# Attention heads taken in pairs: weight transposes, value products and their copies for two heads at once, query products two steps ahead

## The chip, the cores and the metric

The kernel runs on one core of a Trainium2 chip. The metric is the device time of one execution in microseconds (us), lower is better. Five engines with queues of their own work side by side and meet only at semaphores: TensorE (PE; its weight loads are shown apart as PEld), VectorE (DVE), ScalarE (ACT), GpSimd (POOL) and SyncE (SP, which issues most DMAs). Each engine takes its instructions strictly in the order in which they were written.

## The reference

Input x is 16 batches of 256 rows of 512 numbers. Four layers are added to it one after the other: a long convolution with gating, a mixture of experts, cross attention, and a dense feed-forward layer. Only the attention is touched here:

```python
kv_c = kv @ W_kvc                     # 256 x 128 per batch
q_c = q @ W_dq                        # 256 x 192
q_nope = (q_c @ W_uq)                 # 16 heads x 128
q_rope = rope(q_c @ W_qr)             # 16 heads x 64
scores = (q_nope . (kv_c @ W_uk) + q_rope . rope(kv_c @ W_kr)) * scale
scores = where(good, scores, -1e30)   # 8 keys back from the segment id
attn = softmax(scores)
out = (attn . (kv_c @ W_uv)) @ W_o    # summed over the 16 heads
```

## The kernel before, in words

The attention phase folds weights, so that a head needs four steps on TensorE. `scores` multiplies the absorbed query (`qah`, `qal`, 128 rows) and the rotated query (`qr`, a high and a low half) with the keys: ten products into bank `S` for both query tiles. `pturn` transposes the softmax weights `pr` (four transposes into bank `T`). `av` multiplies them with the compressed values (six products into bank `PO`). `vo` multiplies the result with the folded output weight (six products, 512 wide, into the two banks `U`). Every operand is kept as a rounded high part and a low part: ScalarE copies the bank into the high part, VectorE subtracts it from the bank to get the low part (`pth`/`ptl`, `oth`/`otl`, `qah`/`qal`). So each step on TensorE is followed by a copy on ScalarE and, behind it, one subtraction on VectorE.

The queries are prepared beside this. `qabs(P)` makes the absorbed queries of two heads (ten products). `qrot(Q, t)` makes the rotated queries of four heads for one query tile: five products, three multiplications on VectorE and an addition on GpSimd. `qrot2` splits the sum into `rr` (a copy on ScalarE, then a subtraction on VectorE), and `qturn` transposes `rr` (four transposes) and ScalarE copies the result to `qr`.

The order is written out by hand in one loop over N = 16 b + h (b the batch, h the head, 256 steps and four to drain). Each step issues, in this order: `qrot2` where it is due, `scores(N)` (with VectorE's masked minimum `L1224` and ScalarE's exponent `L1228` for two tiles), `qrot` where it is due, `vo(N-4)`, the preparation of the next batch (lists `Bq`), `normalise(N)` (`L1234`, `L1235`), `pturn(N-1)`, `av(N-2)`, `wprep` (only in the first eight steps), and the list `C` with `qturn` and `qabs`. The preparation of batch b+1 in step h: statistics at 0 and 1, normalising at 1 and 2, transposes at 2 and 3, the mask at 4 (eight VectorE instructions), `keys` at 5, `values` at 6, `krope` at 7, `qcomp` at 9; GpSimd mixes the input of batch b+2 (`mix`, four long instructions) after steps 12 and 14. The output of a batch is added on VectorE (`L1275`) at step 3 of the next.

Three PSUM banks (`M0` to `M2`) are handed out in turn by `take()`; whoever takes one waits for the release by the taker three before. The last steps also start the dense layer (`next(dense)`). The conversion of the weights to head factors (`wprep`) fills the start of the attention, where GpSimd mixes batch 1, SyncE stores it, and VectorE's `norm(1, 0)` waits for that store.

Of the kernel before, what the change touches and what calls it, by code (L numbers as in the profile page):

```python
# [926 lines left out]
def attention_phase(nc, ctx, mem, d, front, idx, gat, ident, mhalf, small, batches=B):  # L927
# [282 lines left out]
    def scores(N):  # L1210
# [10 lines left out]
        for t in range(2):  # L1221
# [6 lines left out]
            T["ex", x] = p.do("scalar", lambda e, t=t, k4=k4: e.activation(pr[:, N % 2, t, :], sm[:, k4, :], ACT.Exp, bias=nb[:, k4, 0:1], scale=-1.0,  # L1228
                                                                           accum_out=rw[:, k4, 0:1]), am, g("pt", N - 2), g("rc", x - 4))

    def normalise(N):
# [4 lines left out]

    def pturn(N):
        for kb in range(2):
            for t in range(2):
# [4 lines left out]
        T["pth", N] = p.do("scalar", lambda e: e.activation(pth[:, N % 2, :, :], v, ACT.Copy), a, g("av", N - 2))  # L1244
        T["ptl", N] = p.do("vector", lambda e: e.tensor_tensor(ptl[:, N % 2, :, :], v, f32(pth[:, N % 2, :, :]), ALU.subtract), T["pth", N], g("av", N - 2))  # L1245

    def av(N):
        b, h = divmod(N, NH)
        s = b % 2
        i = 0  # L1250
        for kb in range(2):
# [4 lines left out]
        T["av", N] = a
        v = PO[:, 256 * (N % 2):256 * (N % 2) + 256]
        T["oth", N] = p.do("scalar", lambda e: e.activation(oth[:, N % 3, :], v, ACT.Copy), a, g("vo", N - 3))
        T["otl", N] = p.do("vector", lambda e: e.tensor_tensor(otl[:, N % 3, :], v, f32(oth[:, N % 3, :]), ALU.subtract), T["oth", N], g("vo", N - 3))
# [20 lines left out]
    prf = pr[:, :, :, :].rearrange("p a b c -> p (a b c)")  # L1280
# [104 lines left out]
    T["pt", -1] = T["pt", -2] = T["f", 7]  # L1385
    total = batches * NH
    for N in range(total + 4):
        b, h = divmod(N, NH)
        A, Bq, C = [], [], []
# [19 lines left out]
        for f in A:  # L1409
            f()  # L1410
# [315 lines left out]
```

How the kernel before makes its waits and increments, by code:

```python
    def emit(self, e, eng):  # L72
        seen = {}
        def wait(sem, v):
            if seen.get(id(sem), 0) < v:
                eng.wait_ge(sem, v)
                seen[id(sem)] = v
        for sem, v in self.before:
            wait(sem, v)
        for fn, waits, inc in self.q[e]:
            for w in waits:
                if w is not None:
                    wait(*w)
            ins = fn(eng) if fn else None
            if inc:
                ins.then_inc(*inc)
# [1616 lines left out]
                def run(eng, e=e):  # L1705
                    for p in phases:
                        p.emit(e, eng)
                    if e == "sync":
                        for sem, v in before:
                            eng.wait_ge(sem, v)
```

## Time and profile before

| | us |
|---|---|
| median of 3 runs | 3246.66 (3245.66 to 3248.66) |
| the profiled execution | 3243.99 |
| its span | 3242.2 |
| TensorE busy over the span | 3145.1 (97%) |
| VectorE busy | 2159.4 (67%) |
| ScalarE busy | 1258.5 (39%) |
| GpSimd busy | 1124.4 (35%) |

The attention runs from 1156.75 (first `scores` product) to 2517.71 (first product of the dense layer). A product on TensorE is pipelined: what one costs is the distance from start to start, not its own duration, which overlaps the next. The same holds in part for VectorE and ScalarE. Waits of an engine that is not the bottleneck cost nothing.

### The profile page before, as it was taken

What the parts mean: (1) busy time and instruction counts of PE and PEld (TensorE: products, weight loads), DVE (VectorE), ACT (ScalarE), POOL (GpSimd) and SP (SyncE); (2) the same over time, 40 slices, a digit from 0 to 9 for tenths busy, and PEclk for the clock granted to TensorE, in tenths of its full rate; (3) what the DMA queues carried; (4) which work ended last, traced back from release to release, by engine and by line L of the source; (5) the groups of instructions that cost most, each with busy time, mean ns of one, the idle gap of its engine ahead of it and who ended that gap; (6) DMA issues with size and microseconds to landing.
All of it is one profiled execution on the core that took longest, in us unless ns stands there. A gap on an engine that the chain in (4) does not pass through costs nothing.

```text
span 3242.2 us, 51534 instructions
## 1 busy us (share of the span) xinstructions
PE 3145.1 (97%) x18517; PEld 2686.6 (83%) x18517; DVE 2159.4 (67%) x5741; ACT 1258.5 (39%) x3041; POOL 1124.4 (35%) x1176
## 2 busy tenths in 40 slices
PE   7999999999999789999999999999999999999999
PEld 4666666688899669999999999999999788888887
DVE  6888888755555568888877787777788533333332
ACT  2333333333344345555555555555555311111111
POOL 6877777625344322222222222222211111001110
PEclk9999999999999899999999999999999999999999
DMA  4445443259777731111111111111110300000000
GB/s 128 147 140 149 130 130 102 78 177 335 224 228 230 240 103 53 47 40 40 47 47 36 44 47 47 47 46 47 40 34 21 114 33 26 27 27 26 26 14 14
DMA packets 129418, 285.92 MB, mean 88 GB/s; under 512 B 18840, under 2 KB 19488, under 8 KB 129168
## 3 DMA queue, kind: packets, MB, share of 16 engines
q1 hardware_dynamic: 100080, 186.49, 18.3%
q0 software_dynamic: 29088, 96.13, 9.0%
q8 instruction: 153, 2.51, 0.3%
q14 instruction: 97, 0.79, 0.1%
HBM read 177.98 MB, written 104.58 MB: 87 GB/s over the span
## 4 chain that ended last, share of the span: by engine, by line
PE 78%; DVE 10%; POOL 7%; DMA 2%; ACT 1%; issue 1%; SPq 0%; POOLq 0%; DVEq 0%
PE g_O L1533 11%; PE g_PH L1514 11%; PE t_U L1266 10%; PE t_S L1218 9%; PE t_PO L1253 5%; PE t_M L1202 5%; POOL c_kf L355 3%; PE t_T L1240 3%; PE f_Y L893 3%; PE f_Y L664 2%; PE t_M L1157 2%; PE f_Y L387 2%; PE f_Y L382 2%; DVE c_R L400 2%; DVE c_z L394 2%; PE t_M L1139 2%
## 5 line engine op out<-in xcount | busy, mean ns | idle before, releaser
L1228 ACT ACTIVATE t_pr<-t_sm,t_nb 128x256 f32<-128x256 f32 x512 | 256.5, 502 | 375.0 <-DVE t_nb L1224 375.0
L1172 POOL TENSOR_TENSOR t_r<-t_r 128x256 f32<-128x256 f32 x128 | 96.0, 750 | 779.9 <-DVE t_rw L1234 452.0
L1523 DVE CAST g_hh<-g_hf 128x512 fp32r<-128x512 f32 x128 | 62.2, 486 | 414.5 <-PE g_O L1533 413.0
L1533 PE MATMUL g_O<-g_w,g_hh 128*128 128x512 f32 x1024 | 335.9, 389 | 0.0
L1514 PE MATMUL g_PH<-g_xh,g_w 128*128 128x512 f32 x1024 | 319.8, 394 | 7.0 <-DVE g_w L109 7.0
L355 POOL TENSOR_TENSOR c_kf<-c_vt,c_ct 128x512 f32<-128x512 f32 x256 | 296.4, 1178 | 0.0
L1522 ACT ACTIVATE g_hf<-g_PH,b1g 128x512 f32<-128x512 f32 x128 | 88.3, 690 | 501.7 <-PE g_PH L1514 501.7
L1235 DVE TENSOR_SCALAR t_pr<-t_pr,t_rw 128x256 f32<-128x256 f32 x512 | 222.9, 435 | 18.1
L1514 PEld LDWEIGHTS g_PH<-g_xh,g_w 128*128 128x128 f32 x1024 | 191.0, 189 | 45.8 <-DVE g_w L109 7.4
L1533 PEld LDWEIGHTS g_O<-g_w,g_hh 128*128 128x128 f32 x1024 | 192.2, 188 | 39.9
L387 PE MATMUL f_Y<-c_kh,c_th 128*128 128x512 f32 x448 | 200.1, 447 | 10.4 <-ACT c_kh L362 10.4
L1266 PE MATMUL t_U<-t_voh,t_oth 128*128 128x512 f32 x512 | 202.0, 395 | 0.0
L1266 PE MATMUL t_U<-t_voh,t_otl 128*128 128x512 f32 x512 | 201.9, 394 | 0.0
L1224 DVE CUSTOM_DVE_ANT_0 t_sm<-t_S,t_mk 128x256 f32<-128x256 f32 x512 | 194.8, 417 | 9.2 <-PE t_S L1218 9.2
L1266 PE MATMUL t_U<-t_vol,t_oth 128*128 128x512 f32 x512 | 200.7, 392 | 0.0
L1514 PE MATMUL g_PH<-g_xl,g_w 128*128 128x512 f32 x512 | 200.3, 391 | 0.0
L1533 PE MATMUL g_O<-g_w,g_hl 128*128 128x512 f32 x512 | 199.2, 389 | 0.0
L394 DVE TENSOR_TENSOR c_z<-f_Y,c_ct 128x512 f32<-128x512 f32 x256 | 174.0, 680 | 34.7 <-PE f_Y L382 34.5
L382 PE MATMUL f_Y<-c_kf,c_t 128*128 128x512 f32 x384 | 185.4, 591 | 0.0
L1245 DVE TENSOR_TENSOR t_ptl<-t_T,t_pth 128x512 fp32r<-128x512 f32 x256 | 175.5, 685 | 11.7 <-ACT t_pth L1244 11.6
L400 DVE TENSOR_REDUCE c_R<-c_z 128x64 f32<-128x512 f32 x256 | 174.9, 683 | 6.7
L387 PE MATMUL f_Y<-c_kl,c_th 128*128 128x512 f32 x448 | 178.1, 397 | 0.0
(335 smaller groups left out, 9319.1 us busy)
## 6 DMA issues: line engine op xcount, KB each, us to landing
xs<-c_zero SPq DMA_DIRECT2D x71, 256.0 KB, 5.3
f_xg<-xs SPq DMA_DIRECT2D x71, 256.0 KB, 3.2
ys<-f_yt POOLq DMA_DIRECT2D x71, 256.0 KB, 3.3
c_tr<-kpad SPq DMA_DIRECT2D x60, 256.0 KB, 4.7
f_xg<-xn SPq DMA_DIRECT2D x40, 256.0 KB
c_xt<-x SPq DMA_DIRECT2D x32, 256.0 KB, 3.5
c_cr<-ctx SPq DMA_DIRECT2D x32, 256.0 KB, 3.9
c_ct<-ctxh SPq DMA_DIRECT2D x32, 256.0 KB, 4.4
```

The source lines that it names most:

```text
L355: T["kv", h] = T["kv1", n] = p.do("gpsimd", lambda e: e.tensor_tensor(o, iv, ic, ALU.mult), g("vt", h), g("ct", h), g("kl", n - 8), g("kh" ...
L382: last = p.do("tensor", lambda e, c=c, mb=mb: e.matmul(Y[y % 4][:, :], t0[:, s, c], kf[:, v, mb, :], start=False, stop=mb == lb), g("t0", ...
L387: last = p.do("tensor", lambda e, a=a, b_=b_, c=c, mb=mb, i=i: e.matmul(Y[y % 4][:, :], a[:, s, c], b_[:, v, mb, :], start=(mb == 0 and i ...
L394: T["z", h] = T["z1", y] = p.do("vector", lambda e: e.tensor_tensor(zz.rearrange("p (b j i) -> p b j i", i=8, j=8), iv, ic, ALU.mult), las ...
L400: T["red", y] = T["R", h] = p.do("vector", lambda e: e.tensor_reduce(rr, zr, AXX, ALU.add), g("z1", y), g("pr", h - 2))
L1218: a = p.do("tensor", lambda e, t=t, j=j, q=q, k=k: e.matmul(PS1[:, 256 * t:256 * t + 256], q, k[:, s, :], start=j == 0, stop=j == 4), g("q ...
L1224: T["am", N] = am = p.do("vector", lambda e, t=t, k4=k4: e.tensor_tensor_reduce(out=sm[:, k4, :], in0=PS1[:, 256 * t:256 * t + 256], in1=m ...
L1228: T["ex", x] = p.do("scalar", lambda e, t=t, k4=k4: e.activation(pr[:, N % 2, t, :], sm[:, k4, :], ACT.Exp, bias=nb[:, k4, 0:1], scale=-1. ...
L1235: T["nm", x] = p.do("vector", lambda e, t=t, k4=k4: e.tensor_scalar(pr[:, N % 2, t, :], pr[:, N % 2, t, :], rw[:, k4, 1:2], None, ALU.mult ...
L1266: a = p.do("tensor", lambda e, t=t, tt=tt, j=j, o=o, w=w: e.matmul(PU[t][:, :], o[:, N % 3, tt], w[:, h, :], start=h == 0 and j == 0, stop ...
L1514: T["ph", n] = p.do("tensor", lambda e, kk=kk, a=a, b_=b_, i=i: e.matmul(ph[:, :], a[k][:, kk, :], b_[:, s, kk, :], start=i == 0, stop=i = ...
L1533: tk = p.do("tensor", lambda e, a=a, b_=b_, t=t, fin=fin, c=c, beg=beg: e.matmul(O[t][:, :], a[:, n % 2, c], b_[k], start=beg, stop=fin), ...
```

## The change

The softmax weights get three buffers instead of two. At every even step N the weight transposes of heads N-2 and N-1 are issued together (the second head's into one of the three shared banks), directly behind the rotated queries' four transposes. `av` runs at every odd step for two heads at once, six products 512 wide in place of twelve 256 wide, with one copy and one subtraction 512 wide in place of two each. `qrot`, `qrot2`, `qturn` and `qabs` move ahead by one or two steps, `qcomp` goes to step 7 and `krope` to step 8; before the loop `qrot(1, 0)`, `qrot(1, 1)` and `qabs(1)` are added, which the loop then lacks. The steps of the dense layer come one step later.

```diff
-    oth = m.sb("oth", [128, 3, 256], F32R)
-    otl = m.sb("otl", [128, 3, 256], F32R)
+    oth = m.sb("oth", [128, 2, 256], F32R)
+    otl = m.sb("otl", [128, 2, 256], F32R)
+    pr = m.sb("pr", [128, 3, 2, 256])
...
     def pturn(N):
+        i = N % 2
+        bank, pi, pf = take() if i else (PT1, None, g("ptl", N - 2))
         for kb in range(2):
             for t in range(2):
-                a = p.do("tensor", ... e.transpose(PT1[...], pr[:, N % 2, t, ...], ident),
-                         g("nm", 2 * N + 1), g("nm", 2 * N), g("ptl", N - 1), c_id, ...)
+                a = p.do("tensor", ... e.transpose(bank[...], pr[:, N % 3, t, ...], ident),
+                         g("nm", 2 * N + 1), g("nm", 2 * N), pf, c_id, ...)
...
+        if i:
+            free_m(pi, T["ptl", N])
     def av(N):
...
-                a = p.do("tensor", ... e.matmul(PO[:, 256 * (N % 2):256 * (N % 2) + 256], k[:, s, kb, :], q[:, N % 2, kb, :], ...
+                a = p.do("tensor", ... e.matmul(PO[:, :], k[:, s, kb, :], q[:, kb, :, :].rearrange("p h c -> p (h c)"), ...
...
-        T["oth", N] = p.do("scalar", ... oth[:, N % 3, :], v ... g("vo", N - 3))
-        T["otl", N] = p.do("vector", ... otl[:, N % 3, :], v ... g("vo", N - 3))
+        T["oth", N] = T["oth", N + 1] = p.do("scalar", ... oth[:, :, :], v ... g("vo", N - 1))
+        T["otl", N] = T["otl", N + 1] = p.do("vector", ... otl[:, :, :], v ... g("vo", N - 1))
...
     qturn(0, 1)
+    qrot(1, 0)
+    qrot2(1, 0)
     qabs(0)
+    qrot(1, 1)
+    qabs(1)
...
+            if 4 * (Q + 2) < total:
+                A += {1: [lambda: qrot(Q + 2, 0)], 2: [lambda: qrot2(Q + 2, 0)], 3: [lambda: qrot(Q + 2, 1)]}.get(r, [])
             if 4 * (Q + 1) < total:
-                A += {0: [lambda: qrot(Q + 1, 0)], 1: [lambda: qrot(Q + 1, 1)]}.get(r, [])
-                if r in (1, 2):
-                    qrot2(Q + 1, r - 1)
-                C += {1: [lambda: qturn(Q + 1, 0)], 2: [lambda: qturn(Q + 1, 1)]}.get(r, [])
-            if N % 2 == 0 and N // 2 + 1 < total // 2:
-                C += [lambda: qabs(N // 2 + 1)]
+                A += {0: [lambda: qrot2(Q + 1, 1)]}.get(r, [])
+                D += {0: [lambda: qturn(Q + 1, 0)], 2: [lambda: qturn(Q + 1, 1)]}.get(r, [])
+            if N % 2 and N + 3 < total:
+                C += [lambda: qabs((N + 3) // 2)]
...
-  ... 7: [lambda: krope(b + 1)], 9: [lambda: qcomp(b + 1)],
+  ... 7: [lambda: qcomp(b + 1)], 8: [lambda: krope(b + 1)],
...
+        if N % 2 == 0:
+            for f in D:
+                f()
+            if 0 <= N - 2 < total:
+                pturn(N - 2)
+                pturn(N - 1)
         if 0 <= N - 4 < total:
             vo(N - 4)
         for f in Bq:
             f()
         if N < total:
             normalise(N)
-        if 0 <= N - 1 < total:
-            pturn(N - 1)
-        if 0 <= N - 2 < total:
-            av(N - 2)
+        if N % 2 and 0 <= N - 3 < total:
+            av(N - 3)
```

Three places where this moves instructions. TensorE, step h = 10 of a batch, from the end of its scores on. Before, the transposes stand behind `vo` and the value products (L1253) directly behind them:

```order
L1218 MATMUL t_S<-t_krl,t_qr 128x256
L1266 MATMUL t_U<-t_voh,t_oth 128x512
L1266 MATMUL t_U<-t_voh,t_otl 128x512
L1266 MATMUL t_U<-t_vol,t_oth 128x512
L1266 MATMUL t_U<-t_voh,t_oth 128x512
L1266 MATMUL t_U<-t_voh,t_otl 128x512
L1266 MATMUL t_U<-t_vol,t_oth 128x512
L1240 MATMUL t_T<-ident,t_pr 128x128 [waits t_vector]
L1240 MATMUL t_T<-ident,t_pr 128x128 x3
L1253 MATMUL t_PO<-t_pth,t_kvh 128x256 [waits t_scalar,t_vector]
```

Now twelve transposes stand in a row ahead of `vo` (L1272), four of rotated queries, eight of weights:

```order
L1218 MATMUL t_S<-t_krl,t_qr 128x256
L1187 MATMUL t_M<-t_identr,t_rr 128x128 x4
L1243 MATMUL t_T<-ident,t_pr 128x128 x4
L1243 MATMUL t_M<-ident,t_pr 128x128 [waits t_vector]
L1243 MATMUL t_M<-ident,t_pr 128x128 x3
L1272 MATMUL t_U<-t_voh,t_oth 128x512 [waits t_vector,t_scalar]
```

The value products have left the even step; they stand in the odd one, ahead of the query products.

VectorE, the whole of step h = 10. Before, from the masked minima (L1224) through normalising to the low parts of weights, values and queries:

```order
L1224 ISA t_sm,t_nb<-t_S,t_mk 128x256 [waits t_tensor]
L1224 ISA t_nb 128x1
L1224 ISA t_sm,t_nb<-t_S,t_mk 128x256
L1224 ISA t_nb 128x1
L1234 RECIPROCAL t_rw<-t_rw 128x1 [waits t_scalar]
L1235 TENSOR_SCALAR t_pr<-t_pr,t_rw 128x256 [waits t_vector]
L1234 RECIPROCAL t_rw<-t_rw 128x1 [waits t_scalar]
L1235 TENSOR_SCALAR t_pr<-t_pr,t_rw 128x256 [waits t_vector]
L1245 TENSOR_TENSOR t_ptl<-t_T,t_pth 128x512 [waits t_scalar]
L1259 TENSOR_TENSOR t_otl<-t_PO,t_oth 128x256 [waits t_scalar]
L1207 TENSOR_TENSOR t_qal<-t_M,t_qah 128x512 [waits t_scalar]
```

Now three subtractions that wait for ScalarE stand between the minima and normalising:

```order
L1224 ISA t_sm,t_nb<-t_S,t_mk 128x256 [waits t_tensor]
L1224 ISA t_nb 128x1
L1224 ISA t_sm,t_nb<-t_S,t_mk 128x256
L1224 ISA t_nb 128x1
L1180 TENSOR_TENSOR t_rr<-t_r,t_rr 128x4x64 [waits t_gpsimd,t_scalar]
L1248 TENSOR_TENSOR t_ptl<-t_T,t_pth 128x2x256 [waits t_scalar]
L1248 TENSOR_TENSOR t_ptl<-t_M,t_pth 128x2x256 [waits t_scalar]
L1234 RECIPROCAL t_rw<-t_rw 128x1
L1235 TENSOR_SCALAR t_pr<-t_pr,t_rw 128x256 [waits t_vector]
L1234 RECIPROCAL t_rw<-t_rw 128x1
L1235 TENSOR_SCALAR t_pr<-t_pr,t_rw 128x256 [waits t_vector]
```

The low parts of values and queries have moved to the odd step, whose order is minima, rotated-query multiplications, normalising, `otl`, `qal`. On ScalarE the even step is now two exponents, the `rr` copy, the `qr` copy, two `pth` copies:

```order
L1228 ACTIVATE t_pr,t_rw<-t_sm,t_nb 128x256 [waits t_vector] x2
L1179 ACTIVATE t_rr<-t_r 128x4x64 [waits t_gpsimd]
L1190 ACTIVATE t_qr<-t_M 128x4x128 [waits t_tensor]
L1247 ACTIVATE t_pth<-t_T 128x2x256 [waits t_tensor]
L1247 ACTIVATE t_pth<-t_M 128x2x256 [waits t_tensor]
```

Before, the same step had the two exponents, one `pth`, one `oth`, then `qr` and `qah`, each behind the TensorE work of its own step.

GpSimd at the start of the attention: the additions of rotated queries (L1172), the gathers (L1032) and the mixing of batch 1 (L1045, L1046), with the lines that move:

```order
 L1172 TENSOR_TENSOR t_r<-t_r 128x256 x2
 L1032 DMA t_xT<-ys,idx 128x512 x2
-L1045 TENSOR_SCALAR t_xT<-t_xT,gat 128x512
...
+L1172 TENSOR_TENSOR t_r<-t_r 128x256 x2
+L1045 TENSOR_SCALAR t_xT<-t_xT,gat 128x512
```

Two additions now stand ahead of the mixing of batch 1.

## Rows read from the trace of the kernel before

**Rows 1.** Windows: us; busy of each engine (instructions); granted clock; DMA share; GB/s.
```profile
1256.50:1340.90 84.40, 83.95 (x608) 78.18 (x607) 67.58 (x227) 45.43 (x127) 23.47 (x23) 1.00 0.16 51
```

**Rows 2.** Waits of PE from 1260 to 2434: total us, times, longest.
```profile
PE t_M L1187 <- DVE t_rr L1180: 2.0, 4, 0.5
```

**Rows 3.** Chain of work, in order of time: start us, us, what.
```profile
1706.32 1.73 PE t_M L1100 x8
...
2431.03 1.18 PE t_S L1218 x10
2432.21 1.38 PE t_U L1266 x6
2433.59 0.44 PE t_T L1240 x4
2434.03 0.71 PE t_PO L1253 x6
```

**Rows 4.** Timeline of PE: start us, us, engine, line, out<-in, count.
```profile
1603.26 0.46 PE L1187 MATMUL t_M<-t_identr,t_rr 128*128 128x128 f32 x4
1603.55 0.35 PE L1218 MATMUL t_S<-t_kch,t_qah 128*128 128x256 f32 x1
1603.74 0.28 PE L1218 MATMUL t_S<-t_kch,t_qal 128*128 128x256 f32 x1
```

**Rows 5.** Timeline of DVE, a step h = 1.
```profile
1600.72 0.42 DVE L1224 CUSTOM_DVE_ANT_0 t_sm<-t_S,t_mk 128x256 f32<-128x256 f32 x1
...
1601.40 0.42 DVE L1166 TENSOR_TENSOR t_r<-t_M,t_cq 128x256 f32<-128x256 f32 x1
...
1602.14 0.54 DVE L1084 TENSOR_SCALAR t_xt<-t_xt,t_ag,t_rs 128x512 f32<-128x512 f32 x1
...
1603.60 0.15 DVE L1234 RECIPROCAL t_rw<-t_rw 128x1 f32<-128x1 f32 x1
...
1604.52 0.68 DVE L1245 TENSOR_TENSOR t_ptl<-t_T,t_pth 128x512 fp32r<-128x512 f32 x1
1605.12 0.41 DVE L1259 TENSOR_TENSOR t_otl<-t_PO,t_oth 128x256 fp32r<-128x256 f32 x1
1605.45 0.41 DVE L1180 TENSOR_TENSOR t_rr<-t_r,t_rr 128x256 fp32r<-128x256 f32 x1
```

**Rows 6.** Timeline of ACT, steps h = 1 and 2.
```profile
1601.18 0.51 ACT L1228 ACTIVATE t_pr<-t_sm,t_nb 128x256 f32<-128x256 f32 x1 [1.13 <-DVE t_nb L1224]
...
1603.46 0.39 ACT L1258 ACTIVATE t_oth<-t_PO 128x256 fp32r<-128x256 f32 x1
1603.75 0.60 ACT L1190 ACTIVATE t_qr<-t_M 128x512 fp32r<-128x512 f32 x1
...
1606.24 0.51 ACT L1228 ACTIVATE t_pr<-t_sm,t_nb 128x256 f32<-128x256 f32 x1 [1.58 <-DVE t_nb L1224]
...
1607.24 0.57 ACT L1093 ACTIVATE t_xT<-t_M 128x512 f32<-128x512 f32 x1
1607.72 0.58 ACT L1244 ACTIVATE t_pth<-t_T 128x512 fp32r<-128x512 f32 x1
```

**Rows 7.** Timeline of DVE, the mask at step h = 4.
```profile
1616.25 0.16 DVE L1066 CAST t_sgf<-t_sgi 128x2 f32<-128x2 int32 x1
...
1616.64 0.72 DVE L1071 TENSOR_SCALAR t_mt<-t_iota,t_sgf 128x256 f32<-128x256 f32 x1
...
1618.19 0.35 DVE L1071 TENSOR_SCALAR t_mt<-t_iota,t_sgf 128x256 f32<-128x256 f32 x1
...
1619.26 0.15 DVE L1234 RECIPROCAL t_rw<-t_rw 128x1 f32<-128x1 f32 x1
```

**Rows 8.** Start of the attention: timelines of POOL, PE and DVE.
```profile
1151.45 1.58 POOL L1045 TENSOR_SCALAR t_xT<-t_xT,gat 128x512 f32<-128x512 f32 x1 [1.07 <-DMA t_xT<-ys,idx]
...
1156.75 0.58 PE L1218 MATMUL t_S<-t_kch,t_qah 128*128 128x256 f32 x1 [1.41 <-DVE t_qal L1207]
...
1170.51 0.74 DVE L1084 TENSOR_SCALAR t_xt<-t_xt,t_ag,t_rs 128x512 f32<-128x512 f32 x1 [0.43 <-DMA x<-t_xt]
```

More of the change, by code:

```diff
@@ L1252, in av @@
             for k, q in ((kvh, pth), (kvl, pth), (kvh, ptl)):
-                a = p.do("tensor", lambda e, kb=kb, k=k, q=q, i=i: e.matmul(PO[:, 256 * (N % 2):256 * (N % 2) + 256], k[:, s, kb, :], q[:, N % 2, kb, :], start=i == 0, stop=i == 5),
-                         g("vl", b), g("vh", b), g("ptl", N), g("pth", N), g("otl", N - 1), g("oth", N - 1), inc=i == 5)
+                a = p.do("tensor", lambda e, kb=kb, k=k, q=q, i=i: e.matmul(PO[:, :], k[:, s, kb, :], q[:, kb, :, :].rearrange("p h c -> p (h c)"), start=i == 0, stop=i == 5),
+                         g("vl", b), g("vh", b), g("ptl", N + 1), g("pth", N + 1), g("otl", N - 1), g("oth", N - 1), inc=i == 5)
                 i += 1
[L1256 to L1259, printed above, removed]
+        T["av", N] = T["av", N + 1] = a
+        v = PO[:, :].rearrange("p (h c) -> p h c", h=2)
+        T["oth", N] = T["oth", N + 1] = p.do("scalar", lambda e: e.activation(oth[:, :, :], v, ACT.Copy), a, g("vo", N - 1))
+        T["otl", N] = T["otl", N + 1] = p.do("vector", lambda e: e.tensor_tensor(otl[:, :, :], v, f32(oth[:, :, :]), ALU.subtract), T["oth", N], g("vo", N - 1))
     def vo(N):
@@ L1265, in vo @@
             for j, (o, w) in enumerate(((oth, voh), (otl, voh), (oth, vol))):
-                a = p.do("tensor", lambda e, t=t, tt=tt, j=j, o=o, w=w: e.matmul(PU[t][:, :], o[:, N % 3, tt], w[:, h, :], start=h == 0 and j == 0, stop=h == NH - 1 and j == 2),
+                a = p.do("tensor", lambda e, t=t, tt=tt, j=j, o=o, w=w: e.matmul(PU[t][:, :], o[:, N % 2, tt], w[:, h, :], start=h == 0 and j == 0, stop=h == NH - 1 and j == 2),
                          g("oth", N), g("otl", N), g("vw", h), g("add", 2 * (b - 1) + t) if h == 0 else None, inc=j == 2)
@@ L1279, in attention_phase @@
     smf = sm[:, :, :].rearrange("p a b -> p (a b)")
[L1280 removed]
+    prf = pr[:, 1:3, :, :].rearrange("p a b c -> p (a b c)")
     xof = xo[:, :, :].rearrange("p a b -> p (a b)")
@@ L1384, in attention_phase @@
     T["ex", -1] = T["ex", -2] = T["ex", -3] = T["ex", -4] = T["f", 6]
-    T["pt", -1] = T["pt", -2] = T["f", 7]
+    T["pt", -2] = T["pt", -1] = T["f", 7]
     total = batches * NH
@@ L1402, in attention_phase @@
                        2: [lambda: turn(b + 1, 0), lambda: norm(b + 1, 1)], 3: [lambda: turn(b + 1, 1)],
-                       4: [lambda: mask(b + 1)], 5: [lambda: keys(b + 1)], 6: [lambda: values(b + 1)], 7: [lambda: krope(b + 1)], 9: [lambda: qcomp(b + 1)],
+                       4: [lambda: mask(b + 1)], 5: [lambda: keys(b + 1)], 6: [lambda: values(b + 1)], 7: [lambda: qcomp(b + 1)], 8: [lambda: krope(b + 1)],
                        }.get(h, [])
@@ L1431, in attention_phase @@
             next(dense)
-        if total - 7 <= N <= total:
+        if total - 6 <= N <= total + 1:
             next(dense, None)
```

21 lines of the change are left out of this document (10 added, 11 removed).

## Prediction

> **What bounds the kernel now.** I read the windows of one batch of the attention first, then who waited, then the chain, then the timelines of each engine. In a batch (16 heads) TensorE is busy 83.95 of 84.40 us, VectorE 67.6, ScalarE 45.4, GpSimd 23.5, at a granted clock of 1.00, the high level of 2.4 GHz [rows 1]. So TensorE's queue is the time, and a batch has at most 0.45 us of its waiting. Named waits are those for `rr` at L1187, 2.0 us in 14 batches [rows 2]. The chain walks from one TensorE group to the next without a piece of another engine between: ten score products 1.18, six of `vo` 1.38, four transposes 0.44, six value products 0.71 [rows 3]. For this the reader should count starts, not durations.
>
> Two ways can move the time: fewer start-to-start distances on TensorE, or new waits in it. The second depends on VectorE and ScalarE, which are not full but whose queues are strict, so the place of a waiting instruction matters.
>
> **The change part by part.**
>
> Value products: twelve of 256 columns, 2 x 0.71 = 1.42, become six of 512. `vo` is such a product, 1.38 for six [rows 3]. That is 0.04 a pair, times 128 pairs: -5 us (bounds -3 to -7, if a product with one bank as target is 0.01 faster or slower). The Trainium skill ("TensorE: Matmul & The Clock Gate", Back-to-back issue gap) gives each product its columns at the full clock and a small fixed part; by that rule two halves cost only 2.5 ns more than one whole, 2 us over all pairs, and the forecast would be 3 us later. The rows have 0.236 for two halves against 0.230, and I go by them.
>
> Joins: behind the rotated queries' transposes the first score product takes 0.19 to its follower (1603.55 to 1603.74) where ten take 1.18, 0.12 each [rows 3, 4]; 0.07 are lost at each of 128 such places. Now weight transposes follow. No row shows that join, so it is 0 to -9; I take -4.5. The weight transposes themselves stay 1024 at 0.11 [rows 3].
>
> Copies: `oth` and `otl` for two heads are 512 wide once instead of 256 wide twice. ScalarE has 0.49 for 512 columns (1603.75 to the next copy's place, 1607.24 to 1607.72 gives 0.48) against 2 x 0.29 [rows 6]; VectorE 0.60 against 2 x 0.33 [rows 5]. That is 0.1 and 0.06 a pair, off TensorE's path: nothing.
>
> Waits removed: `qturn` now uses an `rr` that was made a whole step or two earlier, so the waits of rows 2 go, and with them what GpSimd's mixing causes behind them. 14 batches by 0.45 is 6, by rows 2 it is 2. I take -5.
>
> Waits added, the part that decides. In an even step VectorE has, behind the two minima (0.68, from 1600.72 to 1601.40 [rows 5]), three subtractions that wait for ScalarE. Let the first minimum start at A. ScalarE's first exponent starts at A+0.46 (1600.72 to 1601.18 [rows 5, 6]) and two take 1.00 (1606.24 to 1607.24), the `rr` copy then starts at A+1.46 and lasts 0.41 as `oth` about does, 0.29 to the next start, `qr` 0.49, `pth` 0.48 and its end 0.58 after its start [rows 6]. So VectorE does `rr` at A+1.9, waits, does the first `ptl` at A+2.87, the second by A+4.09, and normalising (0.92, 1603.60 to 1604.52) by A+5.01. It stood idle for 1.9 us of this. The odd step: minima 0.68, rotation 0.74 (1601.40 to 1602.14), normalising 0.92, `otl` and `qal` 0.61 each: 3.56. A pair costs VectorE's queue 8.57 us. TensorE's pair is 2.36 scores, 0.29 + 0.88 transposes, 2.76 `vo`, 0.59 rotation (five products), 1.38 values and 1.18 queries (ten products): 9.44. In pairs without other work TensorE still decides, by 0.9.
>
> The next batch's preparation is unevenly spread. VectorE gets statistics at h = 0, normalising and statistics at 1, normalising at 2: twice 1.46 (1602.14 to 1603.60 [rows 5]). At 3 it adds the output, two of 0.6, at 4 it makes the mask, at 5 the keys' low part (0.33, and some 0.75 of waiting for two ScalarE copies). The mask took 3.01 (1616.25 to 1619.26), of it 0.72 for an instruction that takes 0.35 at its second place [rows 7]; the GpSimd addition beside it is gone from step 4, so 2.65. TensorE gets only 0.44, 0.44 and 1.73 (keys) in these six steps [rows 3]. Sums for h = 0 to 5: VectorE 3 x 8.57 + 2.9 + 1.2 + 2.65 + 0.33 + 0.75 = 33.6; TensorE 3 x 9.44 + 2.6 = 30.9. VectorE falls 2.7 behind. What it may fall behind without a wait: A normally lies 1.4 behind the start of the even step's scores (the last query product's end 0.2, the copy 0.6, `qal` 0.6). The odd head's weight transposes come 1.9 behind that start (1.18 + 0.29 + 0.44) and need its normalising, which ends 1.1 before A, so they wait once A passes 3.0. That leaves 1.5 or a little more, so 1.2 of waiting per batch; queued behind it on TensorE are the transposes, `vo` and the next scores. At h = 7 `qcomp`, sixteen products of the keys' kind (eight take 1.73), is 3.5 us of TensorE for one subtraction of 0.6, and VectorE catches up. 14 batches: +17. Bounds: 0.2 per batch (A may reach 3.9, if the softmax copies have more room than I count) to 2.2 (if GpSimd's operations lengthen VectorE's normalising in steps 9 to 15, so that A starts a batch late): +3 to +31. Edits with no price of their own: the third `pr` buffer, the one `oth` pair (its readers, `vo`, stand ahead of `av` in the same step), and the banks, whose takers three before are done by the same walk.
>
> Start: two sets of rotated products and one of query products are issued ahead of the first scores, 20 products or 2.4 us, twice that at the lower clock level; before, TensorE waits 1.41 there for `qal` [rows 8]. They are given back in the last steps, 2.4 less 0.6. On GpSimd two additions now stand ahead of the mixing of batch 1, which began at 1151.45; they need products that start behind the query transposes and are, by my estimate, not done before 1158. So the mixing, its store and VectorE's `norm(1, 0)`, which waited for the store until 1170.51 [rows 8], come some 7 us later. Bounds 0 (covered) to +7; TensorE's own work of these steps (eight weight conversions) covers most, I take +1 for the whole of the start, given back included (-1 to +7).
>
> End: the last two heads' weights are turned together, behind the last normalising. Added behind the last scores are one head's transposes 0.44, its subtraction 0.60, half the wider value group 0.7, and `vo` of both heads, 1.38 more, after the last copy: 3.1. Less than this only if the dense layer's steps between hide some: +3 (0 to +4).
>
> Sum: -5 - 4.5 - 5 + 17 + 1 + 3 = +6.5. Against the profiled execution of 3243.99 (span 3242.2 and 1.8 around it) this is 3250.5. It lies 2.7 below the median of the runs, so 3253 in their terms.
>
> **The rivals.**
>
> Cover holds. No wait arises at the mask: 14 batches x 1.2 go away. For it: VectorE is busy only 80% of a batch [rows 1], and in the trace its lag behind the scores never stopped TensorE. Against: that was with `ptl` behind normalising, not ahead of it. Time: +6.5 - 17 = -10.5, so 3233.5 in the profiled execution's terms and 3236 in the runs'; with the whole join gain (-9 for -4.5) 3232.
>
> Convoy, clearly slower. The even step's serial ScalarE chain and longer normalising keep A late through the whole batch: 2.2 of waiting per batch, and the start shows 5 of its 7. It decides from the point where VectorE's 8 x 8.57 and some 10 of extras, 79 in all, reach TensorE's 83 by waits for GpSimd and ScalarE. Place: L1180 and L1248 on VectorE, L1243 and L1272 on TensorE. Price: +31 - 17 + 4 (the start's 5 for 1) beyond the forecast, 3271. For it speaks the mask's 0.72 in place of 0.35 beside a GpSimd addition [rows 7]: in the changed order such an addition is issued directly ahead of normalising in four odd steps of each batch. The Trainium skill ("SBUF — State Buffer", Who interferes with whom) says that an instruction like normalising and a GpSimd instruction exclude each other, whichever starts second waiting out the other; by that rule these steps lose up to an addition each. Against: those steps have the spare 0.9 a pair.
>
> Nothing to tell. The join stays (0 for -4.5) and the waits at the mask are 0.5 a batch, 7 in all: -5 + 0 - 5 + 7 + 1 + 3 = +1, so 3245 in the profiled execution's terms and 3248 in the runs'. It speaks for this that all savings are of the size of a hundredth of a microsecond per group.
>
> **How the numbers follow.** The forecast, new waits of about 1.2 per batch against small savings, has 0.45 (its own range 3245 to 3262). Cover holds 0.28. Nothing to tell 0.13. Convoy 0.14. A difference of 0.2% (6.5 us) is about what a measurement of this kernel can tell from no change. The forecast's centre lies on that bound, so it splits between slower and same: slower 0.45, same 0.26, faster 0.29. The range 3232 to 3270 takes in the rival of cover and most of the convoy.
>
> **What would show it.** The windows of a batch: about 84.6 us long with TensorE's work at 83.2; waits of TensorE on L1243 and L1272 for VectorE's L1235 and `otl`, in steps 6 and 7 after the mask. VectorE waiting for ScalarE at L1180 and L1248, 1.9 us a pair. The value products at 0.23 from start to start. The first scores near 1159. The forecast is wrong if batches have no waits (then near 3236), or if the waits lie evenly over all steps.

## The result, and the profile after

| | before | changed |
|---|---|---|
| median of nine runs, us | 3245.66 (3244.36 to 3248.66) | 3255.54 (3250.55 to 3258.74) |
| ratio | | 1.003, interval 1.0021 to 1.0039 |
| span of the profiled execution | 3242.2 | 3248.8 |
| from the first factor product to the first score of batch 1 | 146.05 | 153.67 |
| batches 1 to 14 | 1178.07 | 1178.67 |
| first score of batch 15 to the last `vo` | 82.90 | 84.54 |

The change made the kernel 0.3% slower, 9.9 us by the medians (6.8 to 12.7 by the interval), where 6.3 above the median then known were forecast, 3253. The stretches in the table are distances between starts on TensorE, the factor products being those that convert the weights ahead of the attention: 1110.46, 1256.51, 2434.58 and 2517.48 before; 1107.27, 1260.93, 2439.60 and 2524.14 after. They show +7.6, +0.6 and +1.6. The two spans differ by only 6.6, because the phase ahead of the attention, in which nothing was changed, ended 3.2 earlier in this profile; over all profiles of this study the first factor product starts between 1107.3 and 1112.3. Added up, 7.6 + 0.6 + 1.6 = 9.8, as much as the medians differ by. Of the kernel before there is one profile, so the start's 7.6 is less firm than the batches' 0.6: in the second profile of the changed kernel the start takes 154.42.

The windows of one batch and of batches 1 to 14 of the changed kernel, columns as in [rows 1] (the batch there took 84.40 for 608 TensorE instructions):

```profile
1597.61:1681.79 84.18, 83.79 (x561) 75.92 (x559) 66.54 (x219) 42.67 (x118) 23.38 (x23) 1.00 0.14 45
1260.93:2439.60 1178.67, 1173.23 (x7815) 1062.88 (x7813) 930.73 (x3056) 597.41 (x1652) 312.57 (x311) 1.00 0.14 44
```

The busy time gives no hint of what happened; the waits do. In answer to [rows 2], TensorE from 1270 to 2420:

```profile
PE t_M L1243 <- DVE t_pr L1235: 4.4, 15, 0.5
```

The old waits for `rr` are gone. In their place TensorE waits at the weights' transposes of an odd head for its normalising, as this view names it about once a batch. The chain of waits through the place, step 5 into step 6 of batch 6 (start us, us, what):

```profile
1712.61 1.10 ACT t_pr L1228 x4
1713.71 0.27 ACT t_kc L1104
1713.97 0.28 ACT t_kch L1105
1714.25 0.03 issue
1714.28 0.42 DVE t_kcl L1106
...
1714.80 0.35 DVE t_pr L1235
...
1715.26 0.36 DVE t_pr L1235
1715.63 0.04 issue
1715.67 0.66 PE t_M L1243 x4
1716.33 0.03 issue
1716.36 1.62 PE t_U L1272 x6
```

VectorE comes late out of the mask (its last piece starts at 1710.89), does the normalising of step 4, the minima and the rotation, stands for ScalarE's two copies of the keys, and only then normalises. The timeline of TensorE says what the stop costs. An undisturbed place at step 4 first, then step 6:

```profile
1703.57 0.62 PE L1243 MATMUL t_T<-ident,t_pr 128*128 128x128 f32 x4
1704.03 0.60 PE L1243 MATMUL t_M<-ident,t_pr 128*128 128x128 f32 x4
1704.38 0.48 PE L1272 MATMUL t_U<-t_voh,t_oth 128*128 128x512 f32 x1
...
1714.77 0.62 PE L1243 MATMUL t_T<-ident,t_pr 128*128 128x128 f32 x4
1715.67 0.66 PE L1243 MATMUL t_M<-ident,t_pr 128*128 128x128 f32 x4 [0.28 <-DVE t_pr L1235]
1716.36 0.47 PE L1272 MATMUL t_U<-t_voh,t_oth 128*128 128x512 f32 x1
1716.67 0.40 PE L1272 MATMUL t_U<-t_voh,t_otl 128*128 128x512 f32 x1
```

The eight transposes take 0.81 from their start to that of `vo` at step 4 and 1.59 at step 6: +0.78, of which the waits' view names 0.28. At step 2 the same group takes 1.26 (1692.73 to 1693.99): +0.45 without any wait named there in this batch. Over 14 batches these two places cost 17.3, of which the waits' view has 4.4.

The value products in the chain of waits, in answer to the last of [rows 3]: six for two heads take 1.36, where two groups of six took 1.42.

```profile
1238.23 1.38 PE t_U L1272 x6
1239.61 1.36 PE t_PO L1259 x6
1240.97 1.21 PE t_M L1202 x10
```

The start, in answer to [rows 8]:

```profile
1155.06 1.58 POOL L1045 TENSOR_SCALAR t_xT<-t_xT,gat 128x512 f32<-128x512 f32 x1
...
1174.19 0.55 DVE L1084 TENSOR_SCALAR t_xt<-t_xt,t_ag,t_rs 128x512 f32<-128x512 f32 x1 [8.28 <-DMA x<-t_xt]
```

By the profiles' own times mixing begins 3.6 later than before. But the phase ahead ended 3.2 earlier in this profile: counted from the first factor product, mixing begins at 47.8 where it began at 41.0 (1155.06 less 1107.27, 1151.45 less 1110.46), 6.8 later, and batch 1's normalising at 66.9 where it was at 60.1 (7.6 each in the second profile). VectorE stands 8.28 in front of that normalising where it stood 0.43. A factor's subtraction on VectorE (`mb`, L1323) is queued behind it, and TensorE stands for that one:

```profile
1177.24 0.75 PE L1187 MATMUL t_M<-t_identr,t_rr 128*128 128x128 f32 x4 [7.32 <-DVE t_mb L1323]
```

All of the 7.6 lies behind the first score of batch 0. That one stands 46.3 behind the first factor product in both kernels (1156.75 and 1153.53), 48.2 in the second profile of the changed kernel; from it to batch 1 it takes 99.8 before and 107.4, in the second profile 106.2, after the change.

### The profile page after: what moved, and what is told of

It is laid out like the page before. It is cut to its first block, busy times and chain, and to the rows that moved or that the text cites. A ratio compares the mean times of both kernels' runs of the same rounds, so it can differ in the third digit from the quotient of the medians.

```text
span 3248.8 us, 49365 instructions
## 1 busy us (share of the span) xinstructions
PE 3141.1 (97%) x17749; PEld 2649.8 (82%) x17749; DVE 2142.6 (66%) x5613; ACT 1215.5 (37%) x2913; POOL 1123.2 (35%) x1176
## 4 chain that ended last, share of the span: by engine, by line
PE 60%; DVE 22%; ACT 7%; POOL 6%; issue 2%; DMA 2%; SPq 0%; POOLq 0%; DVEq 0%
PE g_O L1547 11%; PE g_PH L1528 11%; PE t_U L1272 5%; PE t_S L1218 4%; POOL c_kf L355 3%; ACT t_pr L1228 3%; PE t_PO L1259 3%; DVE t_ptl L1248 3%; DVE t_pr L1235 3%; PE f_Y L893 3%; PE f_Y L664 2%; PE t_M L1202 2%; PE f_Y L387 2%; PE f_Y L382 2%; DVE t_sm L1224 2%
## 5 line engine op out<-in xcount | busy, mean ns | idle before, releaser
L1172 POOL TENSOR_TENSOR t_r<-t_r 128x256 f32<-128x256 f32 x128 | 96.1, 751 | 842.0 <-DVE t_r L1169 468.7
L1272 PE MATMUL t_U<-t_voh,t_oth 128*128 128x512 f32 x512 | 212.1, 414 | 1.6 <-DVE t_otl L1265 0.6
L1272 PE MATMUL t_U<-t_voh,t_otl 128*128 128x512 f32 x512 | 201.6, 394 | 0.0
L1272 PE MATMUL t_U<-t_vol,t_oth 128*128 128x512 f32 x512 | 201.2, 393 | 0.0
L1224 DVE CUSTOM_DVE_ANT_0 t_sm<-t_S,t_mk 128x256 f32<-128x256 f32 x512 | 194.5, 417 | 0.0
L387 PE MATMUL f_Y<-c_kh,c_tl 128*128 128x512 f32 x448 | 177.9, 397 | 0.0
```

What stands on the lines that cost most here:

```text
L387: last = p.do("tensor", lambda e, a=a, b_=b_, c=c, mb=mb, i=i: e.matmul(Y[y % 4][:, :], a[:, s, c], b_[:, v, mb, :], start=(mb == 0 and i ...
L1224: T["am", N] = am = p.do("vector", lambda e, t=t, k4=k4: e.tensor_tensor_reduce(out=sm[:, k4, :], in0=PS1[:, 256 * t:256 * t + 256], in1=m ...
```

## The experiments

All against the kernel before on the same chip, in three groups, in which its median was 3242.42 (the first four rows), 3243.10 (mask to step 7, query copies, batch 1 prepared later, query transposes) and 3245.52 (the last four); so medians of different groups are compared by their ratios. "Batches" is batches 1 to 14; "start" is from the first factor product to batch 1, from one profile each. Its part ahead of the first score of batch 0 varies between 45.3 and 48.7 though no edit touches it, so differences of a start below some 3 us may be chance.

| edit to the changed kernel | median | ratio to before (interval) | start | batches |
|---|---|---|---|---|
| none, once more | 3254.48 | 1.0039 (1.0025 to 1.0053) | 154.42 | 1178.57 |
| mask halves to steps 10, 13 | 3290.61 | 1.0148 (1.0133 to 1.0164) | 155.71 | 1211.25 |
| statistics a step later | 3259.30 | 1.0048 (1.0034 to 1.0061) | 154.94 | 1184.10 |
| both | 3298.89 | 1.0176 (1.0162 to 1.0190) | 156.40 | 1220.50 |
| mask to step 7 | 3241.99 | 0.9998 (0.9989 to 1.0007) | 151.07 | 1167.50 |
| query copies behind the weights' | 3244.03 | 1.0005 (0.9996 to 1.0014) | 155.26 | 1170.48 |
| batch 1 prepared two steps later | 3252.37 | 1.0027 (1.0018 to 1.0036) | 150.54 | 1179.71 |
| query transposes behind the weights' | 3261.77 | 1.0057 (1.0043 to 1.0071) | 156.98 | 1183.70 |
| mask to 7, statistics spread | 3250.86 | 1.0017 (1.0008 to 1.0026) | 153.29 | 1175.76 |
| batch 1 later, and store behind loads | 3250.02 | 1.0014 (1.0005 to 1.0023) | 150.19 | 1178.65 |
| mask, statistics, batch 1, store | 3246.04 | 1.0003 (0.9994 to 1.0012) | 146.95 | 1175.43 |
| (kernel before) value products in pairs | 3266.01 | 1.0066 (1.0052 to 1.0079) | 149.56 | 1193.52 |

**The changed kernel once more.** 

> The changed kernel once more, unaltered, for a second profile and as the baseline of this group. It should lie 8 to 11 us above the kernel before. The first profile of it (3250.55) shows +4.4 at the start, +0.6 over batches 1 to 14, +1.6 in the last steps. If what lies between it and its median (5 us) is the start (the mixing of batch 1 and its store), this profile shows the first score of batch 1 later than 1260.93 and batches 1 to 14 again 1178.7 long. If it is spread, the batches are longer.

It lies 12.1 above the kernel before, a little beyond the 8 to 11 expected. Batch 1 begins at 1262.13, 1.2 later than in the first profile; the batches agree within 0.1. The start is the part that varies.

**The mask in two halves at steps 10 and 13.**

```diff
-                       4: [lambda: mask(b + 1)], 5: ...
+                       5: ..., 10: [lambda: mask(b + 1, (0,))], 13: [lambda: mask(b + 1, (1,))],
```

> The mask is taken out of step 4; its half for the first 128 queries stands at step 10, the other half at step 13. Theory (the mask makes VectorE late, and TensorE waits for normalising in step 6): the wait at step 6 goes, 0.76 a batch (0.43 of the wait itself, 0.06 and 0.27 around it), so batches 1 to 14 become 10.7 shorter (1168.0) and the wait at step 2, 0.47, stays. Rival (the wait comes from the serial chain through ScalarE in even steps, wherever the mask is): batches unchanged within 2 us, or the waits move to steps 10 to 14.

The wait at step 6 goes as said (the step takes 3.91 in place of 4.66, 10.6 over 14 batches), but 43 us come in its place, so that the batches are 32.6 longer. The rival had named such a move, to steps 10 to 14. TensorE now waits at steps 12, 14, 15 and 2 (here the lines are two further down, L1245 is the weights' transposes):

```profile
PE t_M L1245 <- DVE t_pr L1237: 20.6, 40, 0.8
```

The second half of a batch has next to no room to catch up in. VectorE's timeline there, normalising of step 11 behind GpSimd's addition, in the version with the mask at step 7 (below), and the addition itself:

```profile
1742.05 0.93 DVE L1235 TENSOR_SCALAR t_pr<-t_pr,t_rw 128x256 f32<-128x256 f32 x1
1743.08 0.59 DVE L1235 TENSOR_SCALAR t_pr<-t_pr,t_rw 128x256 f32<-128x256 f32 x1
```
```profile
1742.09 0.74 POOL L1172 TENSOR_TENSOR t_r<-t_r 128x256 f32<-128x256 f32 x1 [5.90 <-DVE t_rw L1234]
```

0.93 and 0.59 where 0.35 is normal. Both engines start at 1742.1; the 0.59 lies beside GpSimd's mixing, which begins at 1742.80. How far VectorE is behind can be read as the distance from the first score of an even step to VectorE's first minimum. Its mean over 14 batches, steps 0, 2, ... 14:

```
changed       1.62 3.13 2.43 3.43 1.44 2.18 2.03 1.70
mask at 7     1.59 3.11 2.44 1.44 1.44 2.19 2.04 1.71
mask halves   2.20 3.73 2.44 1.44 1.44 2.19 3.50 3.82
```

TensorE stops wherever this is above 3.0. From step 10 to 14 it falls by 0.15 and 0.33 a pair and not by 0.9, so a half mask of 1.3 isn't worked off: TensorE pays for it by stops at 12, 14 and 15, and the next batch's step 2 still begins 0.6 later than in the changed kernel.

**Statistics, normalising and transposes of the second half a step later.**

(The lambdas are left out.)

```diff
-  1: [norm(b + 1, 0), stats(b + 1, 1)], 2: [turn(b + 1, 0), norm(b + 1, 1)], 3: [turn(b + 1, 1)],
-  4: [mask(b + 1)],
+  1: [norm(b + 1, 0)], 2: [turn(b + 1, 0), stats(b + 1, 1)], 3: [norm(b + 1, 1)],
+  4: [turn(b + 1, 1), mask(b + 1)],
```

> In steps 1 to 4 the normalising of the second half's input, its statistics and its transposes come a step later (statistics 2, normalising 3, transposes 4), so that step 1 has 0.5 of extra VectorE work in place of 1.6. Theory: the wait at step 2, 0.47 a batch with what hangs on it, goes (-6.6), but step 3 now also has the output's additions, so the wait at step 4 or 6 may grow by up to 0.5: total -6.6 to 0. Rival (step 2 waits for something else than VectorE's queue): step 2 unchanged.

The stop at step 2 is gone in 13 of 14 batches, so it was VectorE's queue. But step 3 has the output's additions too, and step 4 now stops for about 1.1 in every batch, while the stop at step 6 shrinks by 0.2: +5.4 in place of a gain.

**Both edits.** 

> Both edits together: mask halves at steps 10 and 13, statistics a step later. Theory of queue lag: no wait is left in batches 1 to 14, and they take 1178.7 - 17.3 = 1161.4, some 16.7 less than the kernel before's 1178.07; the run then lies at about 3255 - 17 = 3238, 7 below the kernel before. Rival (a fixed cost of the new order that does not depend on the extra work): less than half of it comes.

42 us longer, not 17 shorter. The two costs alone, 32.6 and 5.4, make 38.0; 3.8 come on top.

**The mask at step 7.**

```diff
-                       4: [lambda: mask(b + 1)], 5: ...
-                       7: [lambda: qcomp(b + 1)],
+                       5: ...
+                       7: [lambda: mask(b + 1), lambda: qcomp(b + 1)],
```

> The mask moves from step 4 to step 7, ahead of qcomp's subtraction, where VectorE stands idle 2.0 us in the changed kernel (waiting for ScalarE's copy of the 16 products) and TensorE has 3.45 us of extra work. Theory (queue lag against TensorE's own extra work decides, not the step's number): the wait at step 6 goes, nothing comes in its place, batches 1 to 14 take 1178.6 - 10.7 = 1168. Rival (any 2.65 us on VectorE costs as in the two-halves version, wherever it is): +5 or more, with waits at step 8.

Batches 11.1 shorter, 10.7 expected. The windows of all 14, and VectorE at step 7: of the 2.0 it stood for ScalarE, 0.18 are left, since the mask fills them.

```profile
1261.43:2428.93 1167.50, 1166.93 (x7815) 1062.36 (x7813) 937.54 (x3054) 601.00 (x1652) 313.06 (x310) 1.00 0.14 44
```
```profile
1717.96 0.16 DVE L1066 CAST t_sgf<-t_sgi 128x2 f32<-128x2 int32 x1
...
1721.21 0.69 DVE L1146 TENSOR_TENSOR t_qcl<-t_M,t_qch 128x512 fp32r<-128x512 f32 x1 [0.18 <-ACT t_qch L1145]
```

No stop is left at step 6, and none came at step 8, which the rival had named. The start is 3.4 shorter as well than in the second profile of the changed kernel, but 2.9 of this lie ahead of the first score of batch 0 (45.3 for 48.2), where nothing was changed; the mask of batch 1, at step 7 of batch 0, can have won no more than the rest. The median is 12.5 below the changed kernel's of the group before, in ratios to the kernel before 0.9998 for 1.0039. Twice the stop at step 6 went with the mask: its place is shown as a cause. The next run shows that it isn't the only one.

**Query copies behind the weights' copies.** TensorE's order is kept; in even steps ScalarE and VectorE do `pth` and `ptl` first and `rr`, `qr` behind.

```diff
-            for f in D:
-                f()
+            late = [f() for f in D] + E_
             if 0 <= N - 2 < total:
                 pturn(N - 2)
                 pturn(N - 1)
+            for f in late:
+                f()
```

> TensorE's order is kept. On ScalarE and VectorE the rr pair and the qr copy go behind the weights' copies, in even steps: exponents, pth, pth, then rr and qr; minima, ptl, ptl, then the rr subtraction. Theory (serial ScalarE chain holds VectorE's queue): of the 1.66 us a pair that VectorE stands idle for ScalarE (1.12 + 0.54), 0.45 go, eight times a batch; the waits at steps 2 and 6 go with it: -17 (batches 1 to 14 at about 1162). Rival (the extra work alone decides, 2.65 of mask against room of 1.5): the wait at 6 shrinks by at most 0.4, -5.

Here the mask stands at step 4 again, and both theories had a part. The stops at L1243 are gone from steps 2 and 6, so the serial chain through ScalarE does hold VectorE, whose idle time for `pth` and `rr` fell from 182 to 146 us. But the bank of the query transposes now comes free later: L1157, the next to take it, starts 0.38 and 0.29 late at steps 3 and 7, which is 9.3 over 14 batches. Without them the batches would take 1161.2, where about 1162 were expected. So the stop at step 6 needs both, the mask at step 4 and the chain ahead of normalising; either taken away ends it. (VectorE's first minimum there comes at 2.28 in place of 3.43; with the 0.38 that TensorE itself lost at step 3 it would be 2.66, still below the 3.0.)

**Batch 1 prepared two steps later.**

(The lambdas are left out here too.)

```diff
+                if b == 0:
+                    Bq += {2: [stats(1, 0)], 3: [norm(1, 0), stats(1, 1)],
+                           4: [turn(1, 0), norm(1, 1)], 5: [turn(1, 1)]}.get(h, [])
```

> For batch 1 alone, prepared in steps 0 to 5 of batch 0, statistics, normalising and transposes come two steps later, so that VectorE doesn't stand 8.3 us before the store of the mixed rows has landed. Theory (the late mixing sets the start): batch 1 begins 4 to 8 us earlier than the changed kernel's 1260.9 to 1262.1. Rival (the 20 products and the weight conversions set it): less than 2 earlier. Batches 1 to 14 unchanged at 1178.6.

By the profile's own time batch 1 begins no earlier, by the distance from the first factor product 3.1 to 3.9: less than the theory's 4 to 8, more than the rival's 2. From the first score of batch 0 on it is 2.6 to 3.8. Batches 1 to 14 are 1.0 to 1.1 longer, which wasn't expected and wasn't followed up. VectorE no longer stands. In its place TensorE stands for a factor load, which on SP's queue is behind the store of the mixed rows (queue, then TensorE):

```profile
1174.15 0.38 SPq L1052 DMA_DIRECT2D x<-t_xt  x1
1174.57 0.47 SPq L1312 DMA_DIRECT2D t_xo<-fac  x1
```
```profile
1178.95 0.80 PE L1318 MATMUL t_M<-t_xo 128*128 128x128 f32 x2 [7.92 <-DMA t_xo<-fac]
```

**The same, and the store issued behind two factor loads.**

```diff
         mix(1, 1)
-        keep(1)
...
+            if N == 1:
+                keep(1)
```

> As the version in which batch 1's preparation comes two steps later, and in addition the store of the mixed rows is issued behind the loads of the factors for heads 10 and 11, not ahead of them, on SP's queue. Theory (the late mixing costs twice, once through VectorE, once through SP's queue, where two factor loads stood behind the store until 1174): from the first factor product to batch 1 it takes 150.5 less 4 to 8, that is 143 to 147; median 4 to 8 below that version. Rival (the start is bound by the banks and the conversions): 149 to 151.

Missed: 150.19, no better than 150.54. The number is the rival's (149 to 151), the reason isn't what it named. The load's wait is gone, and a third way shows: the rotation's addition stands behind the same mixing on GpSimd, ScalarE's queue behind that addition, TensorE behind ScalarE.

```profile
1178.63 0.72 POOL L1172 TENSOR_TENSOR t_r<-t_r 128x256 f32<-128x256 f32 x1
```
```profile
1179.38 0.42 ACT L1179 ACTIVATE t_rr<-t_r 128x256 fp32r<-128x256 f32 x1 [5.64 <-POOL t_r L1172]
```
```profile
1180.34 2.08 PE L1325 MATMUL t_M<-t_xo 128*128 128x512 f32 x2 [6.61 <-ACT t_qr L1190]
```

**Query transposes behind the weights' transposes.**

```diff
-            for f in D:
-                f()
             if 0 <= N - 2 < total:
                 pturn(N - 2)
                 pturn(N - 1)
+            for f in D:
+                f()
```

> The rotated queries' transposes stand behind the weights' transposes, directly ahead of vo, as a join from such transposes to products; ScalarE's qr copy with them, so the pth copies come 0.48 earlier. By the joins alone: the 0.07 that the kernel before lost at each of 112 places comes back (8), the 0.026 that the changed kernel has at the first weight transposes goes (3): +5. By the theory of the queue's lag, the earlier ptl frees VectorE 0.48 a pair and takes the waits of steps 2 and 6 away: -17. Together about -12, batches 1 to 14 at 1167, with 0.07 to 0.1 to be seen behind each group of L1187. Rival (waits don't hang on the ScalarE chain): 1183.

17 worse than expected, mainly by the walk over the banks. The joins came back as said:

```profile
1608.40 0.54 PE L1187 MATMUL t_M<-t_identr,t_rr 128*128 128x128 f32 x4
1608.78 0.47 PE L1272 MATMUL t_U<-t_voh,t_oth 128*128 128x512 f32 x1
1609.08 0.39 PE L1272 MATMUL t_U<-t_voh,t_otl 128*128 128x512 f32 x1
```

The first product of `vo` takes 0.30 to its follower where 0.23 is usual, 112 times 0.077 = 8.6. (That L1187 itself takes 0.38 in place of 0.30 is no loss: the last weight transpose ahead of it takes 0.03 in place of 0.11 to its follower.) The waits at L1243 are gone too. But the rotation's products at steps 3 and 7 now take the bank that an odd head's weights had, and wait for its `ptl`; these two steps become 0.83 and 0.53 longer, 19 us over 14 batches:

```profile
PE t_M L1157 <- DVE t_ptl L1248: 12.6, 28, 0.6
```

**Mask at 7 and statistics spread** (second half's statistics at step 2, normalising at 4, transposes at 5).

> The version with the mask at step 7, and in addition statistics of the second half at step 2, its normalising at 4, its transposes at 5. Theory of the lag: the wait at step 2, 0.47 a batch with what hangs on it, goes too, nothing replaces it: batches 1 to 14 at 1161 (1167.5 - 6.2). Rival (as when they were moved to 2 and 3): a wait at step 4, because VectorE has the output's additions at step 3: 1165 to 1170.

The rival was right as to the place; its 1165 to 1170 was too low for the 1175.76. The stop at step 2 went, and two others came: step 4 stops, and the transposes of step 5 wait for the normalising issued just ahead of them. 8.3 worse than the mask at 7 alone.

```profile
PE t_M L1090 <- DVE t_xt L1084: 3.5, 14, 0.3
PE t_M L1243 <- DVE t_pr L1235: 0.8, 3, 0.3
```

**All of it.** 

> The changed kernel with all three: mask at step 7, statistics and normalising spread over steps 0 to 5, batch 1's own two steps later, store behind two factor loads. By the terms added: 3254.5 - 10.7 - 6.2 - 3.5 - 5 = 3229, 14 below the kernel before. If a term doesn't add up (steps 5 to 7 get too full), 3235.

The start adds up (154.4 - 3.4 - 3.9 = 147.1, measured 146.95), in part by luck, given how the stretch ahead of the first score varies; the batches are those of the spread version. As fast as the kernel before, no faster, and 17 above the 3229 expected, since the spread statistics cost 8 where they were priced as a gain of 6, and the store behind the loads won 0.4 of its 5.

**The value products in pairs, in the kernel before.** Six products of 512 columns in odd steps, one copy pair for two heads; the rest as before.

> The kernel before with one part of the change alone: the value products of two heads as six of 512 columns in odd steps, and their copies once for two heads. Everything else (order of queries, weights' transposes each step, joins of 0.07) as before. By the rows: 2 x 12 halves of 0.119 become 0.229, 0.5 a batch and -7 over batches 1 to 14 (1171). Rival: in odd steps the value products wait for otl and ptl of two heads at once, and batches stay at 1178 or grow.

Missed by 22. The rival's stop, for `otl`, is there but small, at step 8. The large one is elsewhere: the query transposes at L1187 stop for `rr` at step 14 in 13 of the 14 batches, 1.45 us each.

```profile
PE t_M L1187 <- DVE t_rr L1180: 18.8, 13, 1.9
PE t_U L1267 <- DVE t_otl L1260: 2.5, 14, 0.2
```

With all stops and joins taken out of both, by starts, TensorE's work is 1158.7 here and 1165.2 in the kernel before: the 6.5 less are there. The part alone loses it to a wait for `rr` that the changed kernel, which makes `rr` earlier, doesn't have.

## Why the prediction was right, point by point

The forecast held: 3253 for 3255.5, slower, and the mechanism that it named ahead of the others, VectorE late behind the mask, is in the trace and was switched off in an experiment. But two errors of opposite sign lie in it, the batches 1.9 too dear and the start 4.8 too cheap. The forecast's first two terms are for all 16 batches, the measured ones for 14.

| term, batches 1 to 14 unless said | forecast | measured |
|---|---|---|
| value products | -5 | -6.7 (1344 x 0.119 = 159.9 to 672 x 0.228 = 153.2) |
| joins | -4.5 | -5.1 (8.0 gone at L1187; 2.9 new, the first weight transpose takes 0.026 more) |
| waits removed | -5 | -4.9 |
| waits added | +17 | +17.3 |
| sum of these | +2.5 | +0.6 (as the lengths show) |
| start, without what is given back | +2.8 | +7.6 |
| last steps, with the 1.8 given back | +1.2 | +1.6 |
| all | +6.5 | +9.8 |

**Waits added.** Size, cause and place held. The limit that was worked out, a first minimum 3.0 behind the scores, is where TensorE stops: it does at 3.13 and 3.43 and doesn't at 2.43. Two details failed. Of 1.23 a batch, 0.77 are at step 6 and 0.46 at step 2, behind the statistics and normalising of the next batch's input in step 1; the forecast put all on the mask. It had L1272 stop too, and steps 6 and 7; L1243 alone stops, at 2 and 6. VectorE's even step came as worked out: `rr`, the two `ptl` and their end at 1.89, 2.85 and 4.06 behind the first minimum (1683.38, 1685.27, 1686.23, 1687.44) for 1.9, 2.87 and 4.09 of the forecast. And each stop costs 0.33 beyond its idle time, which the forecast didn't know: the idle alone is 0.58 a batch by starts. So 17 for 17.3 is in part luck.

**VectorE catches up.** This step was mis-sized for the second half of a batch: "TensorE still decides, by 0.9" a pair doesn't hold there. The first normalising of steps 9, 11, 13 and 15 takes 0.93 for 0.35, the second of step 11 0.58; 0.9 less these 0.58 to 0.81 leaves 0.1 to 0.3 of room. The forecast had named the addition ahead of normalising, as a point for the convoy, and then set the spare 0.9 against it. Measured, 0.15 to 0.33 are left, and moving 2.65 of mask there costs 33 more than at step 4. It did no harm to the forecast, since with the mask at step 4 the lag is gone by step 8. The rule of the Trainium skill ("SBUF — State Buffer", Who interferes with whom), that such a pair of instructions waits out one another, agrees with 0.93 beside a GpSimd addition of 0.74 where 0.35 is usual. Who starts second the trace doesn't settle: VectorE's record begins 0.04 ahead of GpSimd's, and still it is VectorE's that is longer.

**Value products.** The step held, the size was somewhat larger. Half and whole now both have rows: 2 x 0.119 against 0.228, 10 ns a product. The rule of the Trainium skill ("TensorE: Matmul & The Clock Gate", Back-to-back issue gap) made it 2.5 ns; the measurement decides against it here.

**Joins.** No row had shown what stands between query transposes and weights' transposes. It is 0.026, near the cheap end.

**Start.** This is the term that was mis-sized. "TensorE's own work of these steps covers most, I take +1" failed: 7.6, and with the products left out that are only moved (2.4), 5.2. The delay of the mixing was the 7 forecast (6.8 from the first factor product on), but it was not covered: the named waits of TensorE from 1110 to 1266 grow from 28.4 to 34.1. The sign "first scores near 1159" didn't come; they are no later in the first profile and 1.9 in the second. The delay acts through three queues, of which the forecast named one: VectorE's normalising behind the store, SP's factor loads behind the store, ScalarE's `rr` behind GpSimd. Taking away the first and then the second won 3.1 to 3.9 and 0.4, since each time the next was nearly as late. That the third is the last of them wasn't tried.

**End.** +3 less what is given back was right within half a microsecond.

The rival "cover holds" priced what the kernel would do without the stops: 3236. The mask at step 7 reached 3242 with 10.7 of their 17.3 gone. From the kernel before of its group, 3243.10, its stretches give 3239 (batches 10.6 shorter, start 5.0 and end 1.6 longer), so up to 3 us remain unexplained. One instruction group in the wrong step cost the change 11 us; with it moved the change is worth nothing clear of noise, since the stop at step 2, the start and the end take what is left.

Open: the profiled executions of the changed kernel lie at the low end of its runs (3250.55 of a median 3255.54); 3.2 of that may be the earlier end of the phase ahead. Its nine runs spread over 8 us, the nine before over 4; but 27 later runs of the kernel before spread over 9, so that need not be the change. A version with the mask at step 7 and batch 1's preparation later would by its terms lie 3 to 4 below 3242; it wasn't run, and none of the twelve is shown to beat the kernel before.

## What to carry to other kernels

When work is moved so that two strict queues run closer together, find the limit of the lag between them in one place and follow it over a whole period. The steps where the other engine has extra work pay it back quickly; elsewhere it went down here by 0.15 to 0.33 a pair. Put side work where its engine already stands idle, as the mask ahead of a subtraction that waits 2 us for a copy: against step 7, where no stop shows, the same 2.65 us cost 11 more at step 4 and 44 more at steps 10 and 13. Count starts to find what a stop costs; the idle time in the waits' view was a quarter of it. And before two profiles are compared at one place, count from a common event: by the profile's own times the mixing here seemed 3.6 late and was 6.8.

## What was not expected of the hardware

- A stop inside a run of TensorE transposes costs more than its idle time. The stopped transpose's follower comes 0.055 later than usual (0.164 for 0.109), and the last one's hand-over to the 512-column product takes 0.27 more: from the start of an odd head's transposes to the second product of `vo` it is 1.00 after a stop (1715.67 to 1716.67) and 0.67 undisturbed. In all 28 places of the changed kernel it lies between 0.99 and 1.00, however long the stop was.
- A long wait of TensorE costs twice. Behind the 7.92 for the factor load (batch 1 prepared later) the granted clock is 0.50, the low level of 1.2 GHz, for 5.4 us of the work that follows, in which 19 matmuls were done; in the next 5.4, at 1.00, there were 38:

```profile
1179.00:1184.40 5.40, 5.40 (x19) 4.37 (x20) 2.02 (x8) 1.04 (x3) 0.15 (x1) 0.50 0.37 117
1184.60:1190.00 5.40, 5.40 (x38) 4.66 (x36) 5.05 (x18) 3.14 (x9) 1.44 (x2) 1.00 0.20 74
```

- GpSimd's addition stretches VectorE's normalising from 0.35 to 0.93: 57 of 448 in batches 1 to 14 of the changed kernel, 56 of them the first of steps 9, 11, 13 and 15. Before, 43 were lengthened so far, some to 1.2 or 1.3 beside mixing too. What all lengthening adds to VectorE is 2.5 us a batch before and 2.9 now.
